# Two cross attentions of a twelve-layer program: keys made two batches ahead, and an order of steps for it

## The reference

```python
q = (x @ Wq + bq).reshape(B, Lq, H, D).transpose(0, 2, 1, 3)
k = (y @ Wk).reshape(B, Ly, H, D).transpose(0, 2, 1, 3)
v = (y @ Wv).reshape(B, Ly, H, D).transpose(0, 2, 1, 3)
q = _l2norm(q) * exp(min(scale_mul_log, log(100)))
k = _l2norm(k)
attn = softmax(einsum('bhqd,bhkd->bhqk', q, k) + attn_bias)
oup = einsum('bhqk,bhkd->bhqd', attn, v)
x = x + oup.transpose(0, 2, 1, 3).reshape(B, Lq, C) @ Wo + bo
```

## Time and profile before

| what | us |
|---|---|
| median of three runs (lowest, highest) | 2603.1 (2599.29, 2604.42) |
| the profiled execution: its time, its span | 2586.07, 2584.3 |
| TensorE, VectorE, ScalarE, GpSimd busy | 2251.3, 1624.8, 1226.7, 809.8 |
| l1x, batches 0 to 7, from the first scores of batch 0 | 374.36 to 737.45 |
| l3x, the same | 1880.58 to 2345.66 |

### The profile page before, as it was taken

The page is one execution under the profiler, slowest core; times in us unless marked ns, Lnnn a source line. Parts: engine busy times, 40 slices in busy tenths (PEclk is TensorE's granted clock), DMA queues, the critical chain, the costliest instruction groups (busy, mean ns, idle before and its releaser), DMA issues. The chain is left out here.

```text
span 2584.3 us, 63716 instructions
## 1 busy us (share of the span) xinstructions
PE 2251.3 (87%) x26802; PEld 1404.9 (54%) x26810; DVE 1624.8 (63%) x3620; ACT 1226.7 (47%) x2095; POOL 809.8 (31%) x655
## 2 busy tenths in 40 slices
PE   7885788888868899999999998798788888878898
PEld 6753545556534556556566655465345555555554
DVE  6976364544439846888888754545765555554577
ACT  3334144445443235555555554665345544443465
POOL 5610132422207020333322300254544343452154
PEclk9997999999989989999999999899899998888999
DMA  4203343233140256766767651232422222120132
GB/s 115 68 1 94 98 138 98 71 111 94 42 148 19 46 120 134 151 136 128 141 125 143 124 93 46 68 104 88 112 91 66 66 66 66 41 65 22 63 92 64
DMA packets 358542, 229.99 MB, mean 89 GB/s; under 512 B 289817, under 2 KB 325490, under 8 KB 358258
## 3 DMA queue, kind: packets, MB, share of 16 engines
q1 hardware_dynamic: 355186, 217.52, 34.4%
q0 software_dynamic: 3072, 8.39, 1.1%
HBM read 114.02 MB, written 0.52 MB: 44 GB/s over the span
## 5 line engine op out<-in xcount | busy, mean ns | idle before, releaser
L100 PE MATMUL PS<-hot 128*128 128x512 f16 x476 | 140.1, 432 | 82.3 <-DVE l0a_g L1119 17.5
L3960 POOL TENSOR_TENSOR l2x_rows<-l2x_rows,l2x_one 128x256 f16<-128x256 f32 (+1 forms) x91 | 90.9, 1025 | 377.2 <-DVE l2x_rows L1507 352.3
L4064 PE MATMUL PS<-l2x_rows,l2x_pth 128*128 128x512 f16 x832 | 200.4, 379 | 1.5 <-DVE l2x_mean L4273 1.5
L3723 DVE CUSTOM_DVE_ANT_0 l1x_junk<-PS,l1x_bias 128x401 bf16<-128x401 f32 (+1 forms) x256 | 133.1, 575 | 82.3 <-PE PS L3377 82.3
L3723 DVE CUSTOM_DVE_ANT_0 l3x_junk<-PS,l3x_bias 128x401 bf16<-128x401 f32 (+1 forms) x256 | 132.8, 574 | 49.4 <-PE PS L3377 49.2
L3595 ACT ACTIVATE l1x_pT<-PS 128x512 f32<-128x512 f32 (+1 forms) x208 | 112.7, 593 | 98.1 <-PE PS L3431 98.0
L3595 ACT ACTIVATE l3x_pT<-PS 128x512 f32<-128x512 f32 x144 | 77.8, 591 | 171.4 <-PE PS L3431 171.4
L4266 DVE TENSOR_TENSOR l2x_pl<-l2x_sc,l2x_ph 128x1664 f16<-128x1664 f32 x64 | 124.7, 1949 | 44.0 <-ACT l2x_ph L4143 43.4
L4251 DVE CUSTOM_DVE_ANT_0 l2x_sc<-PS,l2x_bias 128x1665 f32<-128x1665 f32 x64 | 120.9, 1889 | 36.3 <-issue 35.1
L4161 ACT ACTIVATE l2x_meanT<-PS 128x256 f32<-128x256 f32 x64 | 24.5, 383 | 249.8 <-PE PS L4026 249.8
L4018 PE MATMUL PS<-l2x_kh,l2x_qth 128*128 128x512 f16 (+1 forms) x512 | 132.0, 339 | 1.5 <-issue 1.5
(11 more groups left out here) (865 smaller groups left out, 6038.8 us busy)
## 6 DMA issues: line engine op xcount, KB each, us to landing
l2f_unit<-in_L_ffn_units_dram SPq DMA_DIRECT2D x36, 384.0 KB, 3.0
l3f_unit<-in_L_ffn_units_dram SPq DMA_DIRECT2D x34, 384.0 KB, 3.1
l1x_kst<-l1x_kh SPq DMA_DIRECT2D x128, 100.1 KB, 2.4
l3x_kst<-l3x_kh SPq DMA_DIRECT2D x128, 100.1 KB, 2.4
l2x_rows<-in_ctx_dram SPq DMA_DIRECT2D x8, 1536.0 KB
l1x_ctx<-in_ctx_t_dram SPq DMA_DIRECT2D x7, 1601.0 KB, 7.3
l3x_ctx<-in_ctx_t_dram SPq DMA_DIRECT2D x7, 1601.0 KB, 7.7
l1x_kst<-l1x_kl SPq DMA_DIRECT2D x64, 100.1 KB, 2.5
```

Of the source, the lines that this page charges most:

```text
L100: self.nc.tensor.matmul(self.PS[:, bank, :], self.hot[:, 0:P], self.hot[:], start=True, stop=True)
L3723: last = v.tensor_tensor_reduce(junk[:, slot(it), r * BANK:r * BANK + n], PS[:, 2 * slot(it) + r, 0:n], bias[:, 0 if normed else b % 2, at ...
L3960: last = nc.gpsimd.tensor_tensor(high[:, at], of[:, at], one[0:p, at].unsqueeze(2).unsqueeze(3).to_broadcast([p, i, NC, P]), ALU.mult)
L4064: nc.tensor.matmul(PS[:, ACC, :], pth[:, u % 2, m, :], rows2[:, b % 2, :, :, m, :], start=(m == 0), stop=False)
```

## The change

In a batch `b` the value, maximum and M items still belong to batch `b + 1`, but K, N, I and U now belong to batch `b + 2`: the keys are made in the second half of a batch, held in `kh` and `kl`, and stacked when the next batch begins. The value items move to the first steps, the maxima from step 6 (l1x) or 8 (l3x) on, and the first M from step 20 (l3x) or 18 (l1x) to step 16 or 15. Batch 0 makes the keys of batch 1 as before, by a table of its own (`opening_steps`), and in its last steps those of batch 2 as well (`second_keys`); batches 6 and 7 make none. SyncE stacks first and loads the context of the batch after next behind it. GpSimd splits a context in two halves of keys, each with its own count, and K waits for its half.

```diff
...
     A = [("A", v, j) for v in range(QV) for j in range(NCH)]
     R_, E, O_, P_ = ("R", 0, 0), ("E", 0, 0), ("O", 0, 0), ("P", 0, 0)
+    K_ = [("K", c, j) for c in range(NC) for j in range(NH)]
+    N_ = [("N", c, j) for c in range(NC) for j in range(NH)]
+    I_ = [("I", c, j) for c in range(NC) for j in range(NH)]
+    U_ = [("U", c, j) for c in range(NC) for j in range(NH)]
+    V_ = [("V", c, 0) for c in range(NV)]
+    M_ = [("M", c, 0) for c in range(2)]
     if normed:
-        steps = [[("K", 0, 0)], [("K", 0, 1)], [("N", 0, 0), R_], [("N", 0, 1), ("I", 0, 0)], [("U", 0, 0), ("I", 0, 1), ("V", 0, 0)],
-                 [E, ("U", 0, 1)], [("V", 1, 0)], [("K", 1, 0)], [("K", 1, 1)],
-                 [O_, ("N", 1, 0)], [("N", 1, 1), ("I", 1, 0)], [("U", 1, 0), ("I", 1, 1), ("V", 2, 0)],
-                 [P_, A[0], ("U", 1, 1)], [A[1], A[2]], [("V", 3, 0)], [A[3], A[4]], [A[5]], [A[6]], [A[7], A[8]],
-                 [A[9]], [("M", 0, 0), A[10]], [A[11]], [A[12], A[13]], [A[14], A[15]], [("M", 1, 0)], []]
+        steps = [[V_[0]], [], [R_, V_[1]], [], [E], [V_[2]], [V_[3]], [O_], [A[0]], [A[1], A[2]], [A[3]], [A[4]], [P_, A[5]], [A[6], A[7]],
+                 [K_[0]], [K_[1], A[8]], [N_[0], M_[0]], [N_[1], I_[0], A[9]], [U_[0], I_[1], A[10]], [U_[1], K_[2], A[11]],
+                 [K_[3], A[12]], [N_[2], A[13]], [N_[3], I_[2], A[14], A[15]], [U_[2], I_[3]], [U_[3]], [M_[1]]]
+        opening_steps = [[K_[0]], [K_[1]], [N_[0]], [N_[1], I_[0]], [U_[0], I_[1], V_[0]], [U_[1], K_[2]], [K_[3], V_[1]], [N_[2]],
+                         [N_[3], I_[2], V_[2]], [U_[2], I_[3]], [U_[3], V_[3]], [], [], [], [], [],
+                         [A[0], A[1]], [A[2], A[3]], [A[4]], [A[5], A[6]], [A[7], A[8]], [A[9], A[10]], [M_[0], A[11]],
+                         [A[12], A[13]], [A[14], A[15]], [M_[1]]]
+        second_keys = {18: [K_[0]], 19: [K_[1]], 20: [N_[0]], 21: [N_[1], I_[0]], 22: [U_[0], I_[1], K_[2]], 23: [U_[1], K_[3]],
+                       24: [N_[2]], 25: [N_[3], I_[2], U_[2], I_[3], U_[3]]}
...
     else:
-        steps = [[("K", 0, 0)], [], [("K", 0, 1), R_], [("K", 1, 0)], [E], [("K", 1, 1)], [("V", 0, 0)], [O_], [A[0]], [A[1]],
-                 [("V", 1, 0), A[2]], [A[3]], [P_, A[4]], [("V", 2, 0), A[5]], [A[6]], [A[7]], [("V", 3, 0), A[8]], [A[9]],
-                 [("M", 0, 0), A[10]], [A[11]], [A[12]], [A[13]], [A[14]], [A[15]], [("M", 1, 0)], []]
+        steps = [[V_[0]], [], [R_], [V_[1]], [E], [V_[2]], [V_[3], A[0]], [O_, A[1]], [A[2], A[3]], [A[4]], [A[5]], [A[6]], [P_, A[7]],
+                 [A[8]], [K_[0]], [A[9], M_[0]], [A[10]], [K_[1]], [A[11]], [A[12]], [K_[2]], [A[13]], [A[14]], [A[15], K_[3]], [],
+                 [M_[1]]]
+        opening_steps = [[K_[0]], [], [K_[1]], [K_[2]], [], [K_[3]], [V_[0]], [], [V_[1]], [], [V_[2]], [V_[3]], [], [A[0]], [A[1], A[2]],
+                         [A[3], A[4]], [A[5], A[6]], [A[7], A[8]], [A[9], A[10]], [M_[0], A[11]], [], [A[12]], [A[13]], [A[14]], [A[15]],
+                         [M_[1]]]
+        second_keys = {20: [K_[0]], 22: [K_[1]], 23: [K_[2]], 25: [K_[3]]}
...
-    assert len(steps) == STEPS
+    assert len(steps) == len(opening_steps) == STEPS
     WARM = 3
     OFF_SLOT = "IUQTRFZY"
     def at_step(b, s):
-        of = {"R": b > 0, "E": b > 0, "O": b % 2 == 0 and b > 0, "P": b % 2 == 0 and b > 0}
-        return [(it, b - 1 if it[0] in of else b + 1) for it in steps[s] if of.get(it[0], b + 1 < B)]
+        if b == 0:
+            return [(it, 2) for it in second_keys.get(s, [])] + [(it, 1) for it in opening_steps[s]]
+        of = {"R": b - 1, "E": b - 1, "O": b - 1, "P": b - 1, "K": b + 2, "N": b + 2, "I": b + 2, "U": b + 2}
+        return [(it, of.get(it[0], b + 1)) for it in steps[s] if of.get(it[0], b + 1) < B and (it[0] not in "OP" or b % 2 == 0)]
     prepared = [(it, 0) for it in first]
     tail = [(R_, B - 1), (E, B - 1), (O_, B - 1), (P_, B - 1)]
...
                     load_mask(0)
                 sp.dma_start(w[:, 3, :, :], ins[L + weight["o"] + "_heads"].rearrange("g p n -> p g n")).then_inc(loaded["rest"], 16)
                 sp.dma_start(b_o[:], row(ins[L + ("bo" if normed else "b_proj")]).to_broadcast([P, D])).then_inc(loaded["rest"], 16)
-                for b in range(B):
-                    if b + 1 < B:
-                        sp.wait_ge(ctx_parts, FIRST_CTX + b)
-                        sp.dma_start(ctx32[:], ins["ctx_t"][b + 1].rearrange("(c p) n -> p c n", p=P)).then_inc(ctx_loaded, 16)
-                        if not normed:
-                            sp.wait_ge(bias_made, b + 1)
-                            load_mask(b + 1)
-                    stack(b, 0)
-                    stack(b, 1)
+                def load_ctx(b):
+                    sp.wait_ge(ctx_parts, FIRST_CTX + NH * (b - 1))
+                    sp.dma_start(ctx32[:], ins["ctx_t"][b].rearrange("(c p) n -> p c n", p=P)).then_inc(ctx_loaded, 16)
+                load_ctx(1)
+                for c in range(NC):
+                    stack(0, c)
+                if not normed:
+                    sp.wait_ge(bias_made, 1)
+                    load_mask(1)
+                load_ctx(2)
+                for b in range(B - 1):
+                    for c in range(NC):
+                        stack(b + 1, c)
+                    if b + 2 < B and not normed:
+                        sp.wait_ge(bias_made, b + 2)
+                        load_mask(b + 2)
+                    if b + 3 < B:
+                        load_ctx(b + 3)
                 if later is not None:
-                    sp.wait_ge(ctx_parts, FIRST_CTX + B - 1)
+                    sp.wait_ge(ctx_parts, FIRST_CTX + NH * (B - 1))
                     later.load(sp)
             @block.gpsimd
...
                     pool.wait_ge(ctx_loaded, b * 16)
                     pool.wait_ge(made, number[(LAST_USE, b - 1)] + 1)
                     hold()
-                    link(nc.gpsimd.tensor_tensor(ctxh[:], ctx32[:], one[:].unsqueeze(2).to_broadcast([P, NC, NK]), ALU.mult))
-                    nc.gpsimd.tensor_tensor(ctxl[:], ctx32[:], ctxh[:], ALU.subtract).then_inc(ctx_parts, 1)
-                    pool.wait_ge(ctx_parts, FIRST_CTX + b)
+                    for h, (at, n) in enumerate(halves):
+                        link(nc.gpsimd.tensor_tensor(ctxh[:, :, at:at + n], ctx32[:, :, at:at + n],
+                                                     one[:].unsqueeze(2).to_broadcast([P, NC, n]), ALU.mult))
+                        nc.gpsimd.tensor_tensor(ctxl[:, :, at:at + n], ctx32[:, :, at:at + n], ctxh[:, :, at:at + n],
+                                                ALU.subtract).then_inc(ctx_parts, 1)
+                        pool.wait_ge(ctx_parts, FIRST_CTX + NH * (b - 1) + h + 1)
                     if normed:
                         split_keys(b)
                     else:
...
                             pe.wait_ge(w_parts, 1)
                             pe.wait_ge(ctx_parts, j + 1)
                         else:
-                            pe.wait_ge(ctx_parts, FIRST_CTX + b)
+                            pe.wait_ge(ctx_parts, FIRST_CTX + NH * (b - 1) + j + 1)
                         for i, at, n in pieces(*halves[j]):
                             terms = [(x, y, d) for x, y in ((wh, ctxh), (wh, ctxl), (wl, ctxh)) for d in range(NC)]
                             for m, (x, y, d) in enumerate(terms):
```

## The result

| | median, us | lowest to highest | ratio to before |
|---|---|---|---|
| before | 2603.4 | 2599.3 to 2604.4 | |
| changed | 2642.5 | 2641.5 to 2649.4 | 1.0159, 95% 1.0138 to 1.0179 |

Slower by 39 us, where 6 us faster was forecast, and outside the range. On another chip, where before took 2591.9, the changed kernel took 2620.0 (1.0110, 1.0088 to 1.0133), 28 us more. The experiments ran on three chips, where before's median was 2590.6 to 2592.4; each is compared with before on its own chip, and a difference between two experiments is that of their medians, so up to 2 us of it can be the chips'.

A forecast was written before the change was run, and what follows sets the result against it. TensorE's work, waits and lowered clock were taken to bound l1x and l3x. +10 in l1x and -16 in l3x gave -6, applied to the median 2603.1: 2597 us, range 2578 to 2617.

The forecast's parts named there:

- What bounds the kernel: In l1x and l3x TensorE sets the pace: a batch is its work, its waits and the lower clock's cost.
- The DMA wait goes, wholly: In l3x, TensorE's wait for the DMA stacking key rows, 3.3 us a batch, disappears because rows are stacked as a batch begins.
- l1x's waits: l1x batches 1 to 5: 4.1 us removed, 6.2 added less overlap, +9.5; whole layer +10, bounds -5 and +20.
- l1x's clock: l1x was read as running at full clock before; the forecast has no term for a clock loss there.
- l3x's clock, "I take half of the 19.5 us back, -9.7": l3x batches 1 to 5: longest idle stretch shrinks, so half the low clock's cost returns; bounds 0 and -19.5.
- the price of 0.37: Cost in us of each us at low clock, from comparing l3x batches 2 and 4; 52.7 such us cost 19.5.
- The prediction's own sign of being wrong: Among its listed signs: l3x batches over 62 us with the clock still at 0.9.
- l3x's waits, -6: l3x batches 1 to 5: new waits of 9.1 us and 0.2 for exponentials against 10.6, -1.3 a batch.
- the hand-off: l3x's one key buffer: VectorE's read waits for GpSimd's split, so the fourth K item waits 2.4 us.
- Batch 0 of l3x, +26: l3x's first batch makes a second set of keys, 14.3 us of matmuls plus waits, less a DMA wait: 59 to 85.
- Batch 6: l3x's batch 6 makes no keys; with DMA wait, other waits and 4.8 us of clock gone: 64.7 to 39.5, -25.
- The slower one: Rival: l3x's k32 hand-off keeps the clock low, so the -9.7 is lost; 2612 us, chance 0.27.

The follow-up runs named there:

- second profile of each: Before and the changed kernel unaltered, each profiled once more; the changed one measured 2620.0 us, before's l3x took 470.5 us and l1x 360.4.
- filling or moving that wait: Against l1x changed alone (2611.0 us): keep-busy matmuls ahead of the first M, 2614.4; M ahead of K, 2608.9. Against the changed kernel (2620.0): M a tile later, 2622.8.

## Why the prediction was wrong

- **What bounds the kernel.** Right: nothing but TensorE's waits and its clock moved, and no layer behind or between the two changed by more than 3 us. (What differed ahead of l1x in the first pair of profiles was gone in the second.)
- **The DMA wait goes, wholly.** Right, no wait for it is left.
- **l1x's waits.** Right: +9.5 forecast in batches 1 to 5, +10.5 measured, with the M item at 2.19 us (2.15 forecast); batch 0's waits +2.8 (3.3).
- **l1x's clock.** The first step that failed. The text took l1x at full clock and gave the term no bound; busy time rose by 10.7 us there, 7.1 of it in batches 1 to 5, whose low clock went from 12.8 to 30.8 us (6 and 21 in the second profile of each). A timeline of batch 2 shows it fall behind the M item's wait:

```profile
532.34 0.43 PE L3414 MATMUL PS<-ident,l1x_both 128*65 128x128 f32 x2 [2.19 <-DVE l1x_ticks L3728]
...
534.61 1.03 PE L3373 MATMUL PS<-l1x_ctxh,l1x_wh 128*128 128x512 f16 x2
535.44 1.06 PE L3373 MATMUL PS<-l1x_ctxl,l1x_wh 128*128 128x512 f16 x2
```

  but filling or moving that wait did not bring it back, so this is where it falls, not shown to be why.
- **l3x's clock, "I take half of the 19.5 us back, -9.7".** The step that failed most. Low clock did fall, from 52.7 to 35.7 us, a third. But the price of 0.37 came from one pair of batches and was applied to all. With full-clock work known, before paid 0.22 a us, 11.8 us in all, and the changed kernel 0.39, 13.8. The traces show what lies in the low stretches of batches 1 to 5: in the changed kernel mostly value items (14 us), N items (7) and key items (5), which take up to twice as long (an N item 3.58 us for 1.98), and 3 us of idleness; in before some 37 us of scores, biases, maxima and weights times values, 8.5 of idleness and only 6 of key items. So the low clock that went was the cheap part, and what stayed or came costs 0.39. The price was right for low clock that comes on top (0.37 to 0.39 above), not for taking it away. The term came out at +2 in place of -9.7. The prediction's own sign of being wrong was there: two of the five batches took over 62 us, at clocks of 0.89 and 0.92.

  The Trainium skill's "TensorE: Matmul & The Clock Gate" (section "HAM oscillation — how this bites in real kernels") charges half of the throttled time. The five batches here paid 0.39 and 0.22, so the measured price decides; by the page's, an estimate, the changed kernel's 35.7 us would have cost 17.9 where they cost 13.8.
- **l3x's waits, -6.** Measured -1.8: the hand-off at 2.79 us (2.4), and in the tiles small waits for exponentials and issue, 17.0 us over the layer where before had 11.4. The terms that the prediction lists also add to 9.45 us a batch and not to 9.1, so its own sum was nearer -5.
- **Batch 0 of l3x, +26.** Measured +34.9: waits +14.0 (about +12 forecast), and 6.6 us of clock (0.87, 24 us low) that the sum did not hold. Batch 6 gave back 17.8 and not 25, since its clock stayed low (0.85 where before had 0.90).
- **The rivals.** The slower one named a mechanism that the runs bear out for l3x, the hand-off of k32: a second buffer takes 25.7 us away. It gave 2612 because it priced the clock's return as merely lost, l1x's clock at nothing and batch 0 too small. The range's upper end, 2617, is 14 us above before, what l1x's upper bound (+20, and 20 to 23 came) gives with no clock back in l3x (-6). No bound was put on batch 0 of l3x, on the gain of batch 6 or on a clock in l3x that costs more than before's, and these carried the time beyond it.
